# A two-FFN macaron kernel: the gated sum of the expert outputs is taken batch by batch

## The reference, cut to what is computed

```python
x = x + 0.5 * ffn(layernorm(x))          # x: 4 batches x 512 tokens x 256
x = x + attention(layernorm(x))
x = x + 0.5 * ffn(layernorm(x))

def ffn(x):                               # 12 experts, 3 for each token, hidden 640
    probs = softmax(x @ Wr + br)
    top_vals, top_idx = top_k(probs, 3)
    ew = softmax(top_vals)
    out = zeros_like(x)
    for e in range(12):
        sel = top_idx == e
        w_e = sum(where(sel, ew, 0)) / max(sel.sum(), 1)     # one number for each expert
        h = relu(x @ w1[e] + b1[e]) @ w2[e] + b2[e]
        out = out + sel.any(-1)[..., None] * (w_e * h)
    pooled = out.mean(axis=1)                                 # one row of 256 for each batch
    phi = sigmoid(relu(pooled @ Wp1 + bp1) @ Wp2 + bp2)       # one number for each batch
    return out * (1 - 0.8 * (phi > 0.7))
```

## Time and profile before

| | us |
|---|---|
| median of 3 runs | 853.17 (849.06 to 855.06) |
| the profiled execution's own time | 852.16 |
| its span, first to last instruction | 850.4 |
| busy in the span: PE | 700.3 (82%) |
| busy: DVE | 532.6 (63%) |
| busy: POOL | 422.0 (50%) |
| busy: ACT | 315.0 (37%) |
| chain that ended last, shares of the span | PE 66%, DVE 9%, DMA 8%, issue 7%, POOL 4% |

### The profile page before, as it was taken

How to read it: one execution, slowest core, us unless ns; L and a number is a source line. 1 busy time by engine, 2 the same in 40 slices (tenths; PEclk the granted TensorE clock), 3 DMA queues, 4 the chain that set the end, 5 groups by cost and what they waited for, 6 DMA issues and landing times.

```text
span 850.4 us, 20944 instructions
## 1 busy us (share of the span) xinstructions
PE 700.3 (82%) x6530; PEld 588.5 (69%) x6531; DVE 532.6 (63%) x1085; ACT 315.0 (37%) x704; POOL 422.0 (50%) x302
## 2 busy tenths in 40 slices
PE   1416799899999996759999984169999999999964
PEld 1315697789889885247777763149999999999821
DVE  6895799745555553268888879935555555555505
ACT  3886676433333331032223212334333333333300
POOL 0003588888888876010000100046888888888520
PEclk9999999999999999879999995569999999999977
DMA  9988544655555554610000003043444444444473
GB/s 305 375 301 249 135 75 62 149 94 114 94 112 93 111 93 64 203 50 3 0 0 0 1 2 100 0 136 51 74 74 74 75 75 76 76 75 74 56 204 118
DMA packets 76803, 85.51 MB, mean 101 GB/s; under 512 B 7008, under 2 KB 68448, under 8 KB 76384
## 3 DMA queue, kind: packets, MB, share of 16 engines
q0 software_dynamic: 26880, 36.72, 26.2%
q1 hardware_dynamic: 49888, 48.35, 17.3%
HBM read 50.97 MB, written 34.08 MB: 100 GB/s over the span
## 4 chain that ended last, share of the span: by engine, by line
PE 66%; DVE 9%; DMA 8%; issue 7%; POOL 4%; SPq 3%; ACT 1%; DVEq 0%; ACTq 0%; POOLq 0%
PE PS L796 62%; PE PS L853 3%; POOL expert_sums L528 3%; DMA expert_sums<-zeros 3%; DMA expert_sums<-A,place 2%; POOL A L509 2%; DVE A L1335 2%; DMA W<-w 1%; SPq L432 1%; DMA A<-expert_sums 1%; DMA A<-xn_rows,token 1%; DVE A L1332 1%; DVE A L1555 1%; DVE A L1246 1%; DVE X L1504 1%
## 5 line engine op out<-in xcount | busy, mean ns | idle before, releaser
L796 PE MATMUL PS<-W,A 128*128 (+1 forms) x2228 | 275.1, 279 | 13.0 <-DVE A L1555 7.4
L796 PE MATMUL PS<-A,W 128*128 128x256 f16 (+1 forms) x2356 | 280.6, 278 | 3.7 <-issue 1.4
L509 POOL DMA_INDIRECT A<-xn_rows,token x140 | 177.5, 1268 | 193.6 <-DVE token L1358 125.2
L528 POOL DMA_INDIRECT expert_sums<-A,place x140 | 231.2, 1651 | 65.2 <-issue 40.4
L796 PEld LDWEIGHTS PS<-A,W 128*128 (+1 forms) x2356 | 238.0, 110 | 35.0 <-issue 6.3
L796 PEld LDWEIGHTS PS<-W,A 128*128 128x128 f16 (+1 forms) x2228 | 225.5, 103 | 45.1 <-DVE A L1555 8.3
L706 ACT ACTIVATE A<-PS,b1s 128x256 f32<-128x256 f32 x340 | 131.3, 478 | 179.3 <-PE PS L796 177.6
L1392 DVE CAST A<-A 128x1280 f16<-128x1280 f32 x68 | 56.2, 827 | 197.6 <-ACT A L706 197.5
L1394 DVE TENSOR_TENSOR A<-A 128x1280 f16<-128x1280 f32 x68 | 101.5, 1492 | 2.3
L796 PE MATMUL PS<-A 32*128 32x128 f32 (+3 forms) x1248 | 67.5, 284 | 30.2 <-DVE A L1335 23.3
L699 ACT ACTIVATE A<-PS 128x512 f16<-128x512 f32 x70 | 41.9, 599 | 114.3 <-PE PS L853 114.3
(11 more groups left out here) (162 smaller groups left out, 430.8 us busy)
## 6 DMA issues: line engine op xcount, KB each, us to landing
W<-w SPq DMA_DIRECT2D x24, 640.0 KB, 11.1
A<-expert_sums SPq DMA_DIRECT2D x16, 512.0 KB, 6.0
expert_sums<-zeros SPq DMA_DIRECT2D x2, 2304.0 KB, 18.9
expert_sums<-zeros SPq DMA_DIRECT2D x12, 384.0 KB, 2.7
xn_rows<-A SPq DMA_DIRECT2D x8, 512.0 KB, 7.1
A<-b SPq DMA_DIRECT2D x2, 1536.0 KB, 8.3
A<-xn_rows,token POOLq DMA_INDIRECT x140
expert_sums<-A,place POOLq DMA_INDIRECT x140
```

The source lines that it names most:

```text
L509: nc.gpsimd.indirect_dma_start(XG[q][:, u * D:(u + 1) * D], None, xn_dram[:, :], bass.IndirectOffsetOnAxis(ap=token[:, at:at + 1], axis=0) ...
L528: nc.gpsimd.indirect_dma_start(sums_dram[f][q][:, :], bass.IndirectOffsetOnAxis(ap=place[:, at:at + 1], axis=0), YO[q][:, u * D:(u + 1) * ...
L796: return nc.tensor.matmul(out_, l, r, start=start, stop=stop_, skip_group_check=True)
```

## The change

The combine goes batch by batch. A load now takes all four chunks of one batch; SP issues lane 1's four, ACT issues lane 0's four, after both lanes' scatters have landed. DVE adds the lanes of a batch (`added`), then TensorE sums the batch's tokens with the data stationary (128 x 128) and a single column of ones moving, 8 matmuls a batch (16 instructions), ACT copies the two result columns, and the gate's two layers run for this batch alone before TensorE turns to the next batch. DVE gates and updates each batch whole; after the first FFN it takes the statistics of the batch's first tile right behind. The stores at the end are five instead of eight: batches 0 to 2 whole, batch 3 in halves.

At the start of the blocks TensorE's first layer of block 0 comes ahead of the product that yields the expert weights and of block 1's transposes; ACT and DVE are reordered to match, and the second layer of block 0 comes behind block 2's transposes. In the last block TensorE no longer waits for its own first layer before the second layer of block 33, and the first half of its second layer goes to a bank of PSUM that need not wait for block 33's weighing. The zeros for clearing the sums are runs of 384 numbers (1,536 bytes) instead of 128 (512 bytes). The tables `of_batch` and their set-up go away. In the diff, longer runs of removed lines are left out; they stand in the kernel above.

```diff
-        pooled_rows = A[0:B, 0:D]
+        ZW = 384
+        zeros = A[:, xn_at + T * D:xn_at + T * D + ZW]
+        assert xn_at + T * D + ZW <= AR - SLOT // 2
...
+        LAST = [(b, slice(0, NC)) for b in range(B - 1)] + [(B - 1, slice(0, NC // 2)), (B - 1, slice(NC // 2, NC))]
...
-        sums_t = [[s[0:TOKENS, :].rearrange("(i p) d -> p i d", p=P) for s in lanes] for lanes in sums_dram]
+        sums_t = [[s[0:TOKENS, :].rearrange("(c b p) d -> p c b d", p=P, b=B) for s in lanes] for lanes in sums_dram]
+        Ob = O.rearrange("p (c b) d -> p c b d", b=B)
+        O2b = O2.rearrange("p (c b) d -> p c b d", b=B)
...
-                rows = sums_dram[f][lane].rearrange("(p r) (h d) -> p (r h) d", p=P, d=P)
+                rows = sums_dram[f][lane].rearrange("(p r) d -> p (r d)", p=P).rearrange("p (n d) -> p n d", d=ZW)
                 n = rows.shape[1] // pieces
-                sp.dma_start(rows[:, n * piece:n * (piece + 1)], zeros[:, :].unsqueeze(1).to_broadcast([P, n, P])
+                sp.dma_start(rows[:, n * piece:n * (piece + 1)], zeros.unsqueeze(1).to_broadcast([P, n, ZW])
                              ).then_inc(sums_cleared[f], 16)
...
-                for lane, into in ((1, O2), (0, O)):
-                    sp.wait_ge(y_sent[lane], 16 * W * TURNS[lane] * (f + 1))
-                    for c in range(NC):
-                        tiles = slice(c * B, (c + 1) * B)
-                        sp.dma_start(into[:, tiles, :], sums_t[f][lane][:, tiles, :]).then_inc(sums_in[lane][c], 16)
+                sp.wait_ge(y_sent[1], 16 * W * TURNS[1] * (f + 1))
+                for b in range(B):
+                    sp.dma_start(O2b[:, :, b], sums_t[f][1][:, :, b]).then_inc(sums_in[1][b], 16)
                 if f == 0:
                     sp.wait_ge(x_new, B)
                     sp.dma_start(dmask_s, dmask).then_inc(dmask_in, 16)
...
+            for n, (b, chunks) in enumerate(LAST):
+                sp.wait_ge(x_new, B + n + 1)
+                sp.dma_start(out_t[:, chunks, b], Xc[:, chunks, b]).then_inc(x_out, 16)
+            sp.wait_ge(x_out, 16 * len(LAST))
...
-                    pool.wait_ge(x_new, 2 * B)
...
-            return bank[7 - u][:, 0:D]
+            return bank[6 + u][:, 0:D]
...
+                    if isinstance(b, int) and b == 0:
+                        act.wait_ge(counted, 2 * f + 2)
...
-                    high(1, 1)
                     high_parts(1)
                     for m in range(2):
                         square_sum(10, m)
+                    high(1, 1)
                     relu(0, 0)
+                    for m in range(2):
+                        square_sum(11, m)
+                    high(2, 0)
                     act.wait_ge(b2_in, 16)
                     act.wait_ge(w_ready, 1)
-                    high(2, 0)
-                    for m in range(2):
-                        square_sum(11, m)
...
-                act.wait_ge(hid_psum, f + 1)
-                nc.scalar.activation(phid[:, :], bank[2][:, 0:B], ACT.Relu, bias=bp1_s[:, :]).then_inc(hid_ready, 1)
-                act.wait_ge(phi_psum, f + 1)
-                nc.scalar.activation(gate[:, :], bank[3][:, 0:B], ACT.Exp, bias=bp2_s[:, :],
-                                     scale=-1.0).then_inc(phi_exp, 1)
+                for q in range(2):
+                    act.wait_ge(y_sent[q], 16 * W * TURNS[q] * (f + 1))
+                for b in range(B):
+                    act.dma_start(Ob[:, :, b], sums_t[f][0][:, :, b]).then_inc(sums_in[0][b], 16)
+                for b in range(B):
+                    n = B * f + b + 1
+                    act.wait_ge(pool_psum, n)
+                    nc.scalar.copy(pooled[:, KC * b:KC * (b + 1)], bank[b][:, 0:KC]).then_inc(pool_ready, 1)
+                    act.wait_ge(hid_psum, n)
+                    nc.scalar.activation(phid[:, b:b + 1], bank[4 + b % 2][:, 0:1], ACT.Relu, bias=bp1_s[:, :],
+                                         scale=1.0 / N).then_inc(hid_ready, 1)
+                    act.wait_ge(phi_psum, n)
+                    nc.scalar.activation(gate[:, b:b + 1], bank[6 + b % 2][:, 0:1], ACT.Exp, bias=bp2_s[:, :],
+                                         scale=-1.0).then_inc(phi_exp, 1)
...
-                    matmul(bank[2][:, 0:T * E], ones[:, :], EWS, True, True).then_inc(counted, 1)
+                    matmul(bank[7][:, 0:T * E], ones[:, :], EWS, True, True).then_inc(counted, 1)
...
-                    if tail:
-                        pe.wait_ge(tail_first, len(TAIL) * (f + 1))
-                        pe.sem_inc(layer1, 1)
-                    else:
+                    if not tail:
...
-                    pe.wait_ge(y_ready, f * NB + b + 2)
                     for u in range(W):
+                        if u == 1:
+                            pe.wait_ge(y_ready, f * NB + b + 2)
...
+                    pe.sem_inc(layer1, 1)
                     pe.sem_inc(layer2, 1)
 
                 transposes(0, 0)
+                first(0, 0, (8, None)[f])
                 expert_weights()
                 transposes(1, 1)
...
+                first(1, 1, (12, None)[f])
+                if f == 0:
+                    pe.wait_ge(relu_done, FREE + 1)
+                    norms(1)
+                transposes(2, 0)
+                second(0, 0)
+                transposes(3, 1)
+                if f == 0:
+                    pe.wait_ge(scaled, 2)
+                first(2, 0, (16, None)[f])
+                second(1, 1)
+                first_plain = 1
...
-                if f == 0:
-                    pe.wait_ge(ones_ready, B)
-                for lane, sums in ((1, O2), (0, O)):
+                for b in range(B):
+                    n = B * f + b + 1
+                    pe.wait_ge(batch_added, n)
                     for c in range(NC):
...
+                        for k in range(KC):
+                            ins = matmul(bank[b][:, k:k + 1], Ob[:, c, b, k * P:(k + 1) * P], ones[:, 0:1],
+                                         c == 0 and k == 0, c == NC - 1)
+                    ins.then_inc(pool_psum, 1)
+                    pe.wait_ge(pool_ready, n)
+                    for k in range(KC):
+                        ins = matmul(bank[4 + b % 2][:, 0:1], Wp1_s[:, k, :], pooled[:, KC * b + k:KC * b + k + 1],
+                                     k == 0, k == KC - 1)
+                    ins.then_inc(hid_psum, 1)
+                    pe.wait_ge(hid_ready, n)
+                    matmul(bank[6 + b % 2][:, 0:1], Wp2_b[:, :], phid[:, b:b + 1], True, True).then_inc(phi_psum, 1)
...
             def blocks(f):
                 v = nc.vector
-                dve.wait_ge(w_ready, f + 1)
-                block_scales((slice(0, E // 2), slice(0, E))[f])
+                def expert_weights():
+                    dve.wait_ge(counted, 2 * f + 2)
+                    step(v.tensor_reduce(wexp[:, :], bank[7][:, 0:T * E].rearrange("p (i e) -> p e i", e=E), AX.X,
+                                         ALU.add))
+                    step.settle()
+                    v.tensor_tensor(wexp[:, :], wexp[:, :], cntm, ALU.mult).then_inc(w_ready, 1)
+                    dve.wait_ge(w_ready, f + 1)
+                    block_scales((slice(0, E // 2), slice(0, E))[f])
...
                 low(0, 0)
+                if f == 0:
+                    low_parts(1)
                 low(1, 1)
-                if f == 0:
-                    low_parts(1)
+                expert_weights()
                 split(0, 0)
...
-                Oc = O.rearrange("p (c b) d -> p c (b d)", c=NC)
-                O2c = O2.rearrange("p (c b) d -> p c (b d)", c=NC)
-                for c in range(NC):
+                def added(b):
                     for lane in range(LANES):
...
+                        dve.wait_ge(sums_in[lane][b], 16 * (f + 1))
+                    v.tensor_tensor(Ob[:, :, b], Ob[:, :, b], O2b[:, :, b], ALU.add).then_inc(batch_added, 1)
+
+                def gated(b):
+                    g = gate[:, b:b + 1]
+                    dve.wait_ge(phi_exp, B * f + b + 1)
+                    step(v.tensor_scalar(g, g, 1.0, None, ALU.add))
+                    step.settle()
+                    step(v.reciprocal(g, g))
+                    step.settle()
+                    step(v.tensor_scalar(g, g, 0.7, -0.4, ALU.is_gt, ALU.mult))
+                    step.settle()
+                    step(v.tensor_scalar(g, g, 0.5, None, ALU.add))
+                    step.settle()
+                    for chunks in ([slice(0, NC)] if f == 0 else [c for n, c in LAST if n == b]):
+                        v.scalar_tensor_tensor(Xc[:, chunks, b], Ob[:, chunks, b], g, Xc[:, chunks, b],
+                                               ALU.mult, ALU.add).then_inc(x_new, 1)
+                    if f == 0:
+                        dve.wait_ge(x_new, b + 1)
+                        step(v.bn_stats(stats[:, b, :], X[:, b, :]))
+
+                added(0)
+                for b in range(B):
```

(6 more changed lines are left out.)

87 lines of the change are left out of this document (5 added, 82 removed).

## The result

The changed kernel takes 863.72 us (median of 4 runs, 861.68 to 865.57) against 853.5 for the kernel before in the same series: ratio 1.0122, 95% interval 1.0093 to 1.0152. It is slower, as forecast (865, range 851 to 870). The profiled execution took 864.77 us, its span is 863.0.

A forecast was written before the change was run, and what follows sets the result against it. The chain that ended last is two thirds TensorE's work, in the combines through the 64 column sums. 8.8 + 5.0 - 0.5 - 0.2 = +13.1 us on the profiled 852.2 gave 865.3; forecast 865 us, range 851 to 870.

The forecast's parts named there:

- Which clock: PE in both combines: granted clock 0.50 for all four batches, 5.8 us a batch against 3.5 at 1.00.
- Rival 1: Both combines: clock rises behind batch 0, later batches cost 3.5 instead of 5.8 us; not slower, 851.5 us; chance 0.10.
- The routing stretch: Second routing, 517 to 523 us: PE busy 6.00 of 6.00 us at clock 0.50, taken as nearest to the batches' sums.
- Price of a pair: Combine's sums and gate on PE: 0.22 us per one-column float32 instruction pair at clock 0.50, bounds 0.20 and 0.24.
- First combine: Combine after the first FFN: Exp 10.2 us later, order behind it 1.4 us less; net +8.8 us, tail's gain included.
- Last combine: Combine at the end: Exp 9.4 us later, fewer updates and stores behind it; net +5.0 us, tail's gain included.
- The tail: Last blocks: PE's pause before block 33's second layer goes, POOL's four last scatters start 1.2 us earlier.
- Zeros: Clearing of the sums: longer runs of zeros end it 0 to 1.2 us sooner, taken as 0.5 us less.
- Order at the start of the blocks: Start of both FFNs' blocks: nothing in the first; 0 to 1.3 us less in the second, taken as 0.2.
- Edits with one answer: Start of both FFNs' blocks: the order edits treated together, nothing in the first FFN and 0.2 us less in the second.

The follow-up runs named there:

- experiment 4: Changed kernel with 72 half-precision matmuls that compute nothing on PE ahead of the first batch in each combine: 861.55 us, ratio 1.0091.
- experiment 3: Changed kernel with loads, additions and sums by batch, but the gate's layers and Exp once for all four batches: 874.56 us, ratio 1.0222.
- experiment 10: Kernel before with the change's tail and zeros, plus 34 matmuls that compute nothing on PE ahead of each combine's old sums: 844.83 us, ratio 0.9882.
- experiment 6: Three runs, each one part of the change alone on the kernel before: tail 852.61 us, zeros 852.94 us, order at the start of the blocks 867.79 us.
- experiment 5: Kernel before with every part of the change except the combine: median 866.06 us, three executions at 866.0 to 867.7 and one at 852.1.
- experiment 2: Changed kernel with half of the column sums left out, 8 instructions instead of 16 a batch: 853.43 us, ratio 0.9991.
- experiment 8: Kernel before with the changed order alone, and POOL's gathers in the second FFN cut to 64 of 128 rows: 854.08 us, ratio 0.9997.

## Why the prediction held, point by point

- **Which clock.** The step that carried most, and right: 0.50 in both combines over all four batches (first fence). Experiment 4 shows more than the prediction needed: even up beforehand, the clock did not outlast the first batch. Rival 1 falls with it: 15.14 of 18.40 us busy at 0.50, and in experiment 3 13.80 of 13.80. That rival took the Trainium skill at its words (TensorE: Matmul & The Clock Gate, Part 1): the gate is set by how busy PE has lately been; these two stretches do not agree with it. The routing stretch of the earlier trace rows gave the right clock, though its instructions are transposes and not sums. In experiment 10 the old sums, with 256 moving columns, kept 1.00 for 14.20 us.
- **Price of a pair.** Taken as 0.22 us with 0.15 of latency; 3.57 us for sixteen gives (3.57 - 0.15) / 16 = 0.21, and a batch 5.62 us instead of 5.8 ((373.46 - 356.61) / 3 from the Exps of batches 0 and 3, at 356.61 and 373.46). From PE's first sum to the end of the last Exp that is 22.9 us instead of 23.5 (four batches and an Exp): 0.6 us less than forecast in each combine.
- **First combine**, +10.0 forecast from the last scatter on, +9.38 measured: the batches' 0.6, PE starting some 0.4 us sooner after the scatter than forecast, and behind the gate a gain of 1.0 instead of 1.4 (the Exp to the attention, 6.23 before, 5.22 after).
- **Last combine**, +6.2 forecast, +4.60 measured. The Exp moved by 9.29 us relative to the last scatter (25.44 before, 34.73 after), forecast 10.6: 0.6 from the batches, 0.7 from an earlier start. From the Exp's start to the end 5.16 us remain of 9.85, forecast 5.5 (0.3 for the Exp and 5.2 behind it).
- **The tail**: 1.22 us in each FFN, forecast 1.2; alone it is worth 2.3 us in time by the ratio of experiment 6, whose interval reaches from 0.2 to 4.4.
- **Zeros.** The mis-sized bound: I limited the gain by the 381 GB/s of the earlier trace rows to 1.2 us; stores in runs of 1,536 bytes move at 401, and the first gather comes 1.9 us sooner. It did not matter: with the zeros alone 2.2 of the 2.9 us were given back within the blocks (experiment 6). The forecast -0.5 came out as +1.07, with the order's share in the first FFN in it, but between executions with the same first FFN that time moves by 1.8 us (315.43 to 317.24), so neither sign is shown.
- **Order at the start of the blocks.** "Edits with one answer" was wrong as a step, though its number (nothing, and -0.2) came out near enough in the changed kernel (+0.42 in the second FFN). Alone, the same edit costs 14 us (experiment 6), and with tail and zeros in three executions of four (experiment 5). The prediction saw PE and the gathers but not that POOL's program leaves no slack to TensorE's 6.99 us, so that where its scatters fall beside DVE decides the loop's pace. The range of 851 to 870 would not have held a changed kernel with both costs. That the changed kernel's loop settled in the fast pace was luck as far as the prediction goes: nothing in it gave a reason.
- **What stays open**: why the same order settles in the fast pace with the new combine (by their times all four executions of the changed kernel and all ten of experiment 2) and mostly in the slow one with the old combine or with one gate. In the changed kernel and in experiment 3 the second FFN's third scatter begins at the same distance behind the transposes before it (4.91 and 4.92 us), but DVE's cast begins 6.42 us behind them in the one and 6.06 in the other; the scatter takes 1.61 us in the first and 2.06 in the second. Where that 0.36 comes from I have not found.

## What to carry to other kernels

A reduction that waits for the last data should leave as few TensorE instructions behind that data as it can: the old sums were as many, but half of them ran under the loads, while cutting the work by batch put a full chain of sums, copy, two layers and four hops behind the last landing, four times, at half the clock. Before forecasting an "order only" edit as nothing, add up what every engine does in one period of the loop that follows, and look for one with no slack beside the bound. If TensorE waits long ahead of a burst, work that computes nothing can have the clock up when the burst begins; whether it stays up has to be read from the trace: here it did through 64 sums of 256 moving columns (experiment 10) and did not through the second batch of one-column sums (experiment 4).

## What the runs showed of the hardware that was not expected

- POOL's indirect transfers take 0.98 us (gather) and 1.57 (scatter) in the loop where they do not begin during DVE's 1.49 us subtraction of two SBUF operands, and 1.59 and 2.59 where they do. In the fences of experiment 6 the gather then ends 0.89 us behind the subtraction's end (655.40 and 654.51), the scatter 1.45 (653.82 and 652.37): a little less than they take otherwise, as if held until then. The subtraction itself is never longer, not even in before, where it begins 0.48 us ahead of a scatter's end (653.02 and 653.50):

```profile
L1394 DVE TENSOR_TENSOR A<-A x68: 1491/1492/1494, 79.4 to 799.7; 128x1280 f16<-128x1280 f32 x68
```

  The Trainium skill has a rule that bears on this (SBUF — State Buffer, Who interferes with whom): a DVE instruction with two SBUF inputs contends with a GpSimd (POOL) instruction that reads SBUF, and by the page's account the one that comes second is blocked until the first is done. Where the subtraction came first the durations agree with that; where the scatter came first they do not. That this contention is the cause is argued from the durations, no run takes it away alone. The effect is a loop with two paces, 6.99 and some 7.5 us a block; by its times one kernel can take either (experiment 5).
- A gather of 64 rows costs POOL 0.93 us, one of 128 rows 0.98, at the same place of the loop (experiment 8 and before).
- Zeros stored in packets of 1,536 bytes move at 401 GB/s, of 512 bytes at 348.
- TensorE's granted clock went from 1.00 back to 0.50 in the middle of one-column float32 matmuls (experiment 4, windows), with PE idle by 0.35 us at most between them; 64 of them without a gap stood at 0.50 for 13.80 us (experiment 3).
